# An attention and expert kernel whose front is reordered: dense weights ahead of x's later chunks, one cut on VectorE, DRAM arrays kept by partition

## The chip, the cores and the metric

The kernel runs on one core of a Trainium2 chip. The time is the device time of one execution in microseconds (us). Engines: PE is TensorE (PEld its weight loads), DVE is VectorE, ACT is ScalarE, POOL is GpSimd, SP is SyncE; SPq, ACTq and POOLq are their sequencers, which issue the DMAs.

## The reference

```python
x = L0_attn_x                              # (16, 256, 128)
xn = _layernorm(x, axis=-1)
# attention: 16 heads of 8, LoRA of rank 8 on q, k, v
q, k, v = (xn @ W.T + xn @ Bm.T @ A.T * 2 for each)
s = q k / sqrt(8) + slopes * (i - j) + causal mask
s = (softmax(s) v) @ Wp.T
# experts: 8, the first largest router logit chooses one for each token
h = relu((xn * mask_i) @ W1[i] + b1[i]);  out += h @ W2[i] + b2[i]
return x + s * silu(out)
```

## The kernel before

The 4096 tokens are 32 tiles of 128 rows (NT = 32), two to a batch; there are 16 batches. Five programs, one for each engine, are written out by hand and meet in semaphores; nothing is reordered. A planner (`bank_uses`) only deals out the PSUM banks, four that DVE empties and three that ACT empties, in the order of use.

**Front.** SP loads x in five chunks: tiles 0 to 3, 4 to 7, 8 to 15, 16 to 23, and later 24 to 31 (semaphores x_in0 to x_in4). ACT issues lora and the dense weights (dense_in). PE fills its time with matmuls on zeros (`warm`, line 1127), then forms the LoRA products (line 1132), from which DVE makes w_eff and w_v (line 859). DVE takes each tile's statistics (`moments`, line 796, one instruction a tile) and turns them into rstd and nmr in three groups (`statistics`: tiles 0 to 3, 4 to 15, 16 to 31). Tiles are normalised by DVE, ACT or POOL (NORM_VEC, NORM_ACT, the rest), turned by PE (`turn`, line 1146) and kept (`keep_xT`, ACT line 618 or DVE line 908), projected to q and k (`project`, line 1153) and to v (line 1160).

**Three cuts.** q and k of a batch are cut into three bf16 parts: ACT takes the first (line 624), DVE the remainder (line 847), ACT the second part (line 630), POOL the third (`third_part`, line 503). SP and ACT copy the parts by DMA into qk_stack (lines 409, 371, 377), whose rows also hold constant rows (line 381). Nothing is scored before the last copy of a batch has landed (`stack_ready`).

**Row maxima.** A batch has 11 units (UNITS). For batches 0 and 1 PE scores each unit (lines 1220, 1228) and DVE takes its row maxima (`unit_max`, line 802), with the rest of the statistics, the remainders of batches 2 and 3 and the router logits in between (MOMENTS_FIRST, PROJECT_FIRST, LOGITS_FIRST; `remainder` waits for `project`). In batch 1's run group 2 of the statistics is woven between the maxima (`between`, STATISTICS_FIRST).

**Loop.** Then 16 iterations score batch i (line 1240) and the maxima of batch i+2, exponentiate on ACT (line 741), multiply by v (line 1292), turn and project the result. Meanwhile tokens are ranked by expert; POOL gathers normalised rows from DRAM (line 516) by `from_row`, PE runs 39 expert tiles, and POOL scatters their rows to DRAM (line 530) by `token_of`. At the end SP loads them back, they are gated, multiplied and added to x, and stored (line 452; the last two tiles at line 486).

## Time and profile before

| | us |
|---|---|
| median of 3 runs | 311.3 |
| lowest, highest | 310.02, 312.48 |
| the profiled execution | 307.4 |
| its span in the trace | 305.5 |
| PE busy in the span | 288.2 |
| DVE busy in the span | 214.4 |

The span is the part of the execution that the trace covers; 1.9 us lie around it. All instants below count from its start. A busy PE is not PE at its peak: the columns of a matmul take twice as long at the lower of its two clock levels (1.2 GHz) as at the upper (2.4 GHz).

### The profile page before, as it was taken

How to read it: one execution, taken by the hardware profiler on the slowest of the kernel's cores; microseconds unless marked ns; L12 is line 12 of the kernel's file. 1: busy time of each engine (PE TensorE's matmuls, PEld its weight loads, DVE VectorE, ACT ScalarE, POOL GpSimd, SP SyncE). 2: the span in 40 equal slices, each digit the busy share in tenths (PEclk: the TensorE clock that was granted, in tenths of full speed). 3: DMA queues.
4: the chain of work that ended last, by engine and by line, in shares of the span. 5: the costliest groups of instructions: out<-in, count | busy, mean ns of one | idle time of the engine just before them, and what ended most of it. 6: DMA issues, size and time to landing. Idle time of an engine off the chain costs nothing.

```text
span 305.5 us, 13101 instructions
## 1 busy us (share of the span) xinstructions
PE 288.2 (94%) x5319; PEld 220.9 (72%) x5319; DVE 214.4 (70%) x482; ACT 206.8 (68%) x379; POOL 133.8 (44%) x211
## 2 busy tenths in 40 slices
PE   7989999889798999999999999999999999999893
PEld 3646557758475887888788788878888888876652
DVE  4596897799995665665757576585766667574883
ACT  2343164566568787788778778777778877578981
POOL 3243363114146467646654655655556542141000
PEclk9999999999999999999999999999999999999996
DMA  7689479681224132413313142231414213008532
GB/s 195 164 220 204 122 222 296 217 249 44 59 58 124 47 105 67 118 50 94 81 54 106 51 118 60 76 85 50 123 42 106 79 49 88 28 24 244 146 105 69
DMA packets 46811, 33.89 MB, mean 111 GB/s; under 512 B 5048, under 2 KB 44216, under 8 KB 46624
## 3 DMA queue, kind: packets, MB, share of 16 engines
q1 hardware_dynamic: 42520, 26.80, 32.7%
q0 software_dynamic: 2496, 5.12, 6.1%
q10 hardware_dynamic: 1736, 1.14, 1.7%
q8 instruction: 43, 0.70, 1.0%
q14 instruction: 16, 0.13, 0.1%
HBM read 13.17 MB, written 6.75 MB: 65 GB/s over the span
## 4 chain that ended last, share of the span: by engine, by line
PE 72%; DVE 13%; ACT 4%; DMA 3%; issue 3%; POOL 2%; SPq 1%; ACTq 0%; DVEq 0%; POOLq 0%
PE bank L1342 13%; PE bank L1350 11%; PE bank L1240 11%; PE bank L1292 11%; DVE row_max L802 6%; PE bank L1248 3%; PE bank L1326 3%; PE bank L1153 3%; PE bank L1160 3%; PE bank L1312 3%; DVE w_slots L966 3%; ACT probs L741 2%; PE bank L1334 2%; PE bank L1169 2%; PE bank L1220 2%
## 5 line engine op out<-in xcount | busy, mean ns | idle before, releaser
L802 DVE TENSOR_REDUCE row_max<-bank 128x2 f32<-128x512 f32 (+3 forms) x176 | 105.9, 636 | 21.6 <-PE bank L1228 17.4
L741 ACT ACTIVATE probs<-bank 128x512 f32<-128x512 f32 (+1 forms) x176 | 90.0, 560 | 33.6 <-PE bank L1248 32.9
L1240 PE MATMUL bank<-qk_stack 64*64 64x64 bf16 (+3 forms) x1024 | 60.4, 235 | 3.5 <-DVE row_max L802 1.8
L1220 PE MATMUL bank<-qk_stack 64*64 64x64 bf16 (+3 forms) x1024 | 61.1, 235 | 0.9 <-DMA qk_stack<-parts 0.9
L516 POOL DMA_INDIRECT xs_slot<-normalised_rows,from_row x39 | 38.5, 987 | 41.3 <-PE bank L1248 32.7
L1024 DVE TENSOR_TENSOR hT<-bank,w_slots 128x512 f32<-128x512 f32 x39 | 27.0, 691 | 33.5 <-PE bank L1342 33.5
L530 POOL DMA_INDIRECT expert_rows<-y_slot,token_of x39 | 38.6, 991 | 24.9 <-DVE y_slot L1030 15.0
L1240 PEld LDWEIGHTS bank<-qk_stack 64*64 64x64 bf16 x1024 | 33.9, 107 | 19.7 <-issue 7.3
L717 ACT ACTIVATE w_slots<-w_all 128x1156 f32 x39 | 45.5, 1168 | 3.5 <-issue 1.2
L1292 PE MATMUL bank<-probs,v_diag 128*32 128x64 f32 (+3 forms) x1024 | 45.3, 304 | 0.4 <-issue 0.3
L1342 PE MATMUL bank<-xsT_slot,w_slots 128*128 128x128 f32 x312 | 44.3, 285 | 0.0
L1248 PE MATMUL bank<-cb 64*64 64x128 bf16 (+2 forms) x352 | 43.2, 241 | 0.0
L1228 PE MATMUL bank<-cb 64*64 64x128 bf16 (+2 forms) x352 | 43.0, 241 | 0.0
L1350 PE MATMUL bank<-w_slots,hT 128*128 128x128 f32 x312 | 41.3, 276 | 0.0
L1342 PEld LDWEIGHTS bank<-xsT_slot,w_slots 128*128 128x128 f32 x312 | 37.8, 192 | 2.4 <-issue 0.5
L1350 PEld LDWEIGHTS bank<-w_slots,hT 128*128 128x128 f32 x312 | 38.0, 192 | 0.1
L1220 PEld LDWEIGHTS bank<-qk_stack 64*64 64x64 bf16 x1024 | 33.4, 107 | 5.4 <-issue 5.1
L503 POOL TENSOR_TENSOR parts<-rem,parts 128x512 bf16<-128x512 f32 x16 | 18.5, 1159 | 37.1 <-ACT parts L630 37.1
L1292 PEld LDWEIGHTS bank<-probs,v_diag 128*32 128x32 f32 x1024 | 24.8, 109 | 11.3 <-issue 0.7
L1248 PEld LDWEIGHTS bank<-cb 64*64 64x64 bf16 x352 | 19.7, 107 | 0.0
L1228 PEld LDWEIGHTS bank<-cb 64*64 64x64 bf16 x352 | 19.5, 107 | 0.0
L1127 PE MATMUL bank<-zeros 128*128 128x512 bf16 x49 | 16.6, 444 | 2.3 <-POOL zeros L493 1.0
(134 smaller groups left out, 374.7 us busy)
## 6 DMA issues: line engine op xcount, KB each, us to landing
qk_stack<-parts SPq DMA_DIRECT2D x120, 64.0 KB, 2.0
qk_stack<-parts SPq DMA_DIRECT2D x32, 128.0 KB, 2.4
w_all<-w_experts SPq DMA_DIRECT2D x8, 512.0 KB, 6.0
normalised_rows<-xn_all SPq DMA_DIRECT2D x4, 512.0 KB, 7.2
xn_all<-expert_rows SPq DMA_DIRECT2D x8, 256.0 KB, 5.3
out<-xn_all SPq DMA_DIRECT2D x7, 256.0 KB, 2.3
x_all<-x SPq DMA_DIRECT2D x3, 512.0 KB, 7.5
xs_slot<-normalised_rows,from_row POOLq DMA_INDIRECT x39, 2.9
```

The lines of the kernel that those rows point to most:

```text
L516: pool.indirect_dma_start(xs_slot[:, q % 2, t % 4, :], None, xn_dram[:, :], bass.IndirectOffsetOnAxis(from_row[:, t:t + 1], axis=0)).then_ ...
L530: pool.indirect_dma_start(y_dram[:, :], bass.IndirectOffsetOnAxis(token_of[:, t:t + 1], axis=0), y_slot[:, t % 3, :], None).then_inc(S[f"y ...
L717: act.activation(w_slot[t % 3], w_all[:, bass.ds(e, 1), :].rearrange("p o f -> p (o f)"), ACT.Copy).then_inc(S["w_done"], 1)
L741: act.activation(probs[:, m % PROBS, 0:w], bank[:, 0:w], ACT.Exp).then_inc(emptied, 1)
L802: dve.tensor_reduce(row_max[b % 2][:, n, pairs[0]:pairs[-1] + 1], bank[:, 0:ln_u * len(pairs)].rearrange("p (c k) -> p c k", k=ln_u), AX.X ...
L1220: pe.matmul(bank[to, c * ln_u:(c + 1) * ln_u], q[rows, p, n * BLK:(n + 1) * BLK], k[rows, p, 0:(n + 1) * BLK], start=(c == 0), stop=False, ...
L1228: last = pe.matmul(bank[to, 0:ln_u * len(pairs)].rearrange("p (c k) -> p c k", k=ln_u)[:, :, n * BLK:], ident_b[rows, rows], mask_qk[rows] ...
L1240: pe.matmul(bank[rows, c * ln_u:(c + 1) * ln_u], k[rows, p, kb * BLK:(kb + 1) * BLK], q[rows, p, kb * BLK:], start=(c == 0), stop=False, s ...
L1248: last = pe.matmul(bank[rows, 0:ln_u * len(pairs)].rearrange("p (c k) -> p c k", k=ln_u)[:, :, 0:BLK], ident_b[rows, rows], mask_kq[rows]. ...
L1292: last = pe.matmul(pv_bank[32 * j:32 * j + 32, half * T + kb * BLK:(half + 1) * T], v_diag[b % 2][:, kb, p, :], probs[:, (b * NU + w) % PR ...
L1342: last = pe.matmul(bank[:, c * P:(c + 1) * P], w_slot[t % 3][:, c * P:(c + 1) * P], xsT_slot[:, t // 4 % 2, t % 4, :], start=(c == 0), sto ...
L1350: last = pe.matmul(bank[:, 0:D], hT[:, t % 2, c, :], w_slot[t % 3][:, W2 + c * D:W2 + (c + 1) * D], start=(c == 0), stop=(c == NC_H - 1))
```

## The change

- SP waits for the dense weights before it issues x's chunk 1 and all that stands behind it.
- The constant rows of stack slot 0 are issued by ACT behind normalise(1) instead of at its start; tile 1 is normalised by ACT and tile 2 by DVE.
- `statistics` has one small instruction less in each group.
- PE fills with 12 matmuls instead of 10; w_v is formed last and has its own wait.
- Batch 0's third part goes from POOL to DVE, between the statistics of tiles 10 and 11.
- Tiles 16 to 19 get their statistics ahead of remainder(1); the later ones follow one unit each, so that one is left for batch 1's run, where group 2 starts behind unit 0 instead of unit 4.
- remainder(2) and remainder(3) stand one unit later; ACT's deviation(2) stands ahead of max_rows(0).
- x, out, the normalised rows and the expert rows lie in DRAM by partition: row p * 32 + n instead of n * 128 + p. The ids follow.

```diff
-NORM_VEC, NORM_ACT = (0, 1), (2, 4, 5)
+NORM_VEC, NORM_ACT = (0, 2), (1, 4, 5)
...
-MOMENTS_FIRST = {(0, u): (16 + u,) for u in range(NU)} | {(1, u): (16 + NU + u,) for u in range(16 - NU)}
-STATISTICS_FIRST = 16 - NU
+MOMENTS_FIRST = {(0, u): (20 + u,) for u in range(NU)} | {(1, 0): (31,)}
+STATISTICS_FIRST = 1
...
-    x_tiles = x.rearrange("b (j p) d -> p (b j) d", p=P)
-    out_tiles = out.rearrange("b (j p) d -> p (b j) d", p=P)
+    x_tiles, out_tiles = x, out
...
-    xn_tiles = xn_dram.rearrange("(n p) d -> p n d", p=P)
+    xn_tiles = xn_dram.rearrange("(p n) d -> p n d", p=P)
...
-    y_tiles = y_dram[0:NT * P].rearrange("(n p) d -> p n d", p=P)
+    y_tiles = y_dram[0:NT * P].rearrange("(p n) d -> p n d", p=P)
...
             sp.dma_start(cf[:, 0:P], const_f32[:, 0:P]).then_inc(S["ident_in"], 16)
+            sp.wait_ge(S["dense_in"], 32)
             load_x(1, 4, 8)
...
-            third_part(0)
+            pool.wait_ge(S["part3_done"], 1)
             third_part(1)
...
-            load_const_rows(act, 0, 0, 1)
-
...
-            normalise(2)
+            normalise(1)
+            load_const_rows(act, 0, 0, 1)
             keep_xT(0)
...
             second_part(3)
+            deviation(2)
             max_rows(0)
             first_max_rows()
-            deviation(2)
...
-                follow(dve.tensor_tensor(ln[:, 6, g], ln[:, 6, g], ln[:, 1, g], ALU.mult), group, 5)
-                follow(dve.tensor_scalar(ln[:, 6, g], ln[:, 6, g], -0.5, 1.5, ALU.mult, ALU.add), group, 6)
-                follow(dve.tensor_tensor(rstd[:, g], ln[:, 5, g], ln[:, 6, g], ALU.mult), group, 7)
+                follow(dve.scalar_tensor_tensor(ln[:, 6, g], ln[:, 6, g], -0.5, ln[:, 1, g], ALU.mult, ALU.mult), group, 5)
+                follow(dve.scalar_tensor_tensor(rstd[:, g], ln[:, 6, g], 1.5, ln[:, 5, g], ALU.add, ALU.mult), group, 7)
...
             moments(1, 4, 8)
             remainder(0)
-            then(moments(2, 8, 16))
+            moments(2, 8, 11)
+            dve.wait_ge(S["part2_done"], 1)
+            dve.tensor_tensor(parts[:, 0, 2], rem[:, 0], parts[:, 0, 1], ALU.subtract).then_inc(S["part3_done"], 1)
+            moments(2, 11, 16)
+            then(moments(3, 16, 20))
             remainder(1)
             statistics(1)
...
-                    if b == 0 and u in PROJECT_FIRST:
-                        remainder(PROJECT_FIRST[u])
+                    if b == 0 and u - 1 in PROJECT_FIRST:
+                        remainder(PROJECT_FIRST[u - 1])
...
-            warm(10, vec_bank[3])
+            warm(12, vec_bank[3])
...
             project(1)
+            pe.wait_ge(S["w_eff_done"], 2)
             project_v(0)
```

On SP, the first loads (x_all is x, cf and cb are the constants), before:

```order
L390 DMA x_all<-x 128x4x128
L393 DMA cf<-const_f 128x128
L390 DMA x_all<-x 128x4x128
L395 DMA cb<-const_bf 128x384
L390 DMA x_all<-x 128x8x128
```

and after:

```order
L389 DMA x_all<-x 128x512
L392 DMA cf<-const_f 128x128
L389 DMA x_all<-x 128x512 [waits dense_in]
L395 DMA cb<-const_bf 128x384
L389 DMA x_all<-x 128x1024
```

The loads keep their order, but from the second chunk of x on they stand behind dense_in, and each now moves one run for each partition.

On DVE, from remainder(0) to the first operation of statistics(1) (rem is the remainder, BN_STATS a tile's statistics), before:

```order
L847 TENSOR_TENSOR rem<-bank,parts 128x512 [waits part1_done,vec_full0]
L796 BN_STATS stats<-x_all 128x6 [waits x_in2]
L796 BN_STATS stats<-x_all 128x6 x7
L847 TENSOR_TENSOR rem<-bank,parts 128x512 [waits part1_done,vec_full1,dve_seq]
L820 TENSOR_TENSOR ln<-stats 128x12
```

and after:

```order
L845 TENSOR_TENSOR rem<-bank,parts 128x512 [waits part1_done,vec_full0]
L795 BN_STATS stats<-x_all 128x6 [waits x_in2]
L795 BN_STATS stats<-x_all 128x6 x2
L864 TENSOR_TENSOR parts<-rem,parts 128x512 [waits part2_done]
L795 BN_STATS stats<-x_all 128x6 [waits x_in2]
L795 BN_STATS stats<-x_all 128x6 x4
L795 BN_STATS stats<-x_all 128x6 [waits x_in3]
L795 BN_STATS stats<-x_all 128x6 x3
L845 TENSOR_TENSOR rem<-bank,parts 128x512 [waits part1_done,vec_full1,dve_seq]
```

The third part stands behind the wait for x's chunk 2, and four more tiles' statistics stand ahead of the second remainder.

On DVE, around units 6 and 7 of batch 0's maxima, before:

```order
L802 TENSOR_REDUCE row_max<-bank 128x2 [waits vec_full2]
L796 BN_STATS stats<-x_all 128x6 [waits x_in3]
L847 TENSOR_TENSOR rem<-bank,parts 128x512 [waits part3_done,part1_done,vec_full3]
L802 TENSOR_REDUCE row_max<-bank 128x2 [waits vec_full0]
L796 BN_STATS stats<-x_all 128x6 [waits x_in3]
```

and after:

```order
L801 TENSOR_REDUCE row_max<-bank 128x2 [waits vec_full2]
L795 BN_STATS stats<-x_all 128x6 [waits x_in4]
L801 TENSOR_REDUCE row_max<-bank 128x2 [waits vec_full0]
L795 BN_STATS stats<-x_all 128x6 [waits x_in4]
L845 TENSOR_TENSOR rem<-bank,parts 128x512 [waits part3_done,part1_done,vec_full3]
```

remainder(2) moved behind unit 7's maximum and its statistics, which now read x's last chunk.

## Rows read from the trace of the kernel before

**Rows 1.** The page: busy time of the engines, and the chain by engine.
```profile
PE 288.2 (94%) x5319; PEld 220.9 (72%) x5319; DVE 214.4 (70%) x482; ACT 206.8 (68%) x379; POOL 133.8 (44%) x211
...
PE 72%; DVE 13%; ACT 4%; DMA 3%; issue 3%; POOL 2%; SPq 1%; ACTq 0%; DVEq 0%; POOLq 0%
```

**Rows 2.** The chain of waits, 0 to 20 us: start us, us, what.
```profile
1.39 4.71 DMA dense<-w_dense
...
6.14 1.64 PE bank L1132 x6
7.79 0.96 PE bank L1127 x2
...
9.74 2.06 PE bank L1153 x4
...
12.45 0.64 SPq L409
...
15.73 0.02 SPq L369
...
15.79 2.29 DMA qk_stack<-parts
```

**Rows 3.** PE's timeline: start us, us, line, operation, tiles, count.
```profile
1.01 4.45 PE L1127 MATMUL bank<-zeros 128*128 128x512 bf16 x10 [1.01 <-POOL zeros L493]
...
13.94 3.41 PE L1127 MATMUL bank<-zeros 128*128 128x512 bf16 x15
...
43.20 1.13 PE L1153 MATMUL bank<-xnT_all,w_eff 128*128 128x256 f32 x4
```

**Rows 4.** Windows, 9.5 to 10 us: busy by engine, granted clock, DMA, GB/s.
```profile
9.50:10.00 0.50, 0.36 (x2) 0.29 (x2) 0.06 (x1) 0.46 (x2) 0.00 (x0) 1.00 1.14 297
```

**Rows 5.** The timeline of all engines, 0 to 20 us.
```profile
1.87 1.28 ACTq L381 DMA_DIRECT2D qk_stack<-const_rows  x2
...
6.95 0.16 DVE L836 SCALAR_TENSOR_TENSOR nmr<-ln,rstd 128x4 f32<-128x4 f32 x1
...
13.96 1.16 POOL L503 TENSOR_TENSOR parts<-rem,parts 128x512 bf16<-128x512 f32 x1 [2.59 <-ACT parts L630]
...
15.44 0.69 DVE L847 TENSOR_TENSOR rem<-bank,parts 128x512 f32<-128x512 f32 x1 [0.67 <-ACT parts L624]
...
18.91 0.69 DVE L802 TENSOR_REDUCE row_max<-bank 128x2 f32<-128x512 f32 x1
```

**Rows 6.** The same timeline, 24 to 30 us.
```profile
24.02 0.28 DVE L796 BATCH_NORM_STATS2 stats<-x_all 128x6 f32<-128x128 f32 x1
...
25.29 0.69 DVE L847 TENSOR_TENSOR rem<-bank,parts 128x512 f32<-128x512 f32 x1 [0.98 <-PE bank L1153]
...
26.02 0.62 ACT L630 ACTIVATE parts<-rem 128x512 bf16<-128x512 f32 x1
...
27.86 1.74 POOL L506 TENSOR_SCALAR xn_all<-x_all,rstd,nmr 128x128 f32<-128x128 f32 x4
```

**Rows 7.** The chain in the second run: a tile's statistics, a small operation.
```profile
36.37 0.20 DVE stats L796
...
39.69 0.18 DVE ln L834
```

**Rows 8.** PE's timeline at 44.9 and 48 us: what PE waited for.
```profile
44.90 0.27 PE L1240 MATMUL bank<-qk_stack 64*64 64x192 bf16 x2 [0.23 <-DVE row_max L802]
...
48.05 0.27 PE L1240 MATMUL bank<-qk_stack 64*64 64x192 bf16 x2 [0.58 <-DVE xnT_all L908]
```

**Rows 9.** The page: DMA issues, count, KB each, us to landing; waits for the gathers.
```profile
w_all<-w_experts SPq DMA_DIRECT2D x8, 512.0 KB, 6.0
...
x_all<-x SPq DMA_DIRECT2D x3, 512.0 KB, 7.5
xs_slot<-normalised_rows,from_row POOLq DMA_INDIRECT x39, 2.9
...
  DMA xs_slot<-normalised_rows,from_row: 1.8, 3
```

**Rows 10.** The timeline's last row.
```profile
303.24 0.37 SPq L486 DMA_DIRECT2D out<-xn_all  x1
```

More of the change, by code:

```diff
@@ L855, in _ @@
             dve.wait_ge(S["lora_ps"], 1)
[L856 to L860 removed]
+            for n in range(2):
+                last = dve.scalar_tensor_tensor(w_eff[:, n, :], pv_bank[:, n * P:(n + 1) * P], LORA_SCALE, w_raw[:, n, :], ALU.mult, ALU.add)
             then(last)
             dve.tensor_scalar(w_eff[:, 0, :], w_eff[:, 0, :], float(DH) ** -0.5, None, ALU.mult).then_inc(S["w_eff_done"], 1)
+            dve.scalar_tensor_tensor(w_v[:, :, :], pv_bank[:, 2 * P:3 * P].rearrange("p (a x) -> p a x", a=2), LORA_SCALE,
+                                     w_raw[:, 2, :].rearrange("p (a x) -> p a x", a=2), ALU.mult, ALU.add).then_inc(S["w_eff_done"], 1)
             moments(1, 4, 8)
             remainder(0)
[L865 removed]
+            moments(2, 8, 11)
[3 more added lines that the diff above has]
+            then(moments(3, 16, 20))
             remainder(1)
@@ L971, in keep_ids @@
                 bank, emptied = wait_vec_full(dve, "ids")
-                then(dve.tensor_copy(r40[:, 0, :], bank[:, 0:SLOT_ROWS]))
-                dve.scalar_tensor_tensor(r40[:, 1, :], bank[:, SLOT_ROWS:2 * SLOT_ROWS], float(P), r40[:, 0, :], ALU.mult, ALU.add).then_inc(emptied, 1)
+                then(dve.tensor_copy(r40[:, 0, :], bank[:, SLOT_ROWS:2 * SLOT_ROWS]))
+                dve.scalar_tensor_tensor(r40[:, 1, :], bank[:, 0:SLOT_ROWS], float(NT), r40[:, 0, :], ALU.mult, ALU.add).then_inc(emptied, 1)
                 wait_vec_emptied(dve, "ids")
-                dve.tensor_scalar(from_row[:, :], r40[:, 1, :], -1.0, 0.0, ALU.add, ALU.max).then_inc(S["rows_done"], 1)
+                dve.tensor_scalar(from_row[:, :], r40[:, 1, :], -float(NT), 0.0, ALU.add, ALU.max).then_inc(S["rows_done"], 1)
                 then(dve.scalar_tensor_tensor(r40[:, 0, :], r40[:, 1, :], 0.0, spare_ids, ALU.is_equal, ALU.mult))
-                dve.scalar_tensor_tensor(token_of[:, :], r40[:, 1, :], -1.0, r40[:, 0, :], ALU.add, ALU.add).then_inc(S["tokens_done"], 1)
+                dve.scalar_tensor_tensor(token_of[:, :], r40[:, 1, :], -float(NT), r40[:, 0, :], ALU.add, ALU.add).then_inc(S["tokens_done"], 1)
             def tile_experts():
```

13 lines of the change are left out of this document (4 added, 9 removed).

## The prediction

> **What bounds the kernel now.** I read the page first, then the chain of waits from the start, then the timelines of the engines around it. The page says that PE works 94% of the span and carries 72% of the chain, DVE 13% [rows 1]. The main loop, from about 42 us to 298 us, is therefore PE's and none of its matmuls is touched. What the change can move is the point at which this loop gets going, and the last store. So the question is what ends last in the front.
>
> The chain of the front [rows 2] has three links. The dense weights land at 6.10, then PE does the lora products (6.14, 1.64 us), two filling matmuls, the turns of x and the projection of batch 0 (9.74, 2.06 us). SP issues five copies into the stack from 12.45 on, one after the other, and the last lands at 18.08. Then PE scores and VectorE takes maxima, and up to 48 us the two hold each other.
>
> In the first link PE runs slowly. Ten 128x512 filling matmuls take 4.45 us, 0.44 each, and fifteen of the same shape from 13.94 on take 3.41, 0.23 each; the projection of batch 0 takes 2.06 us and the same pair at 43.20 takes 1.13 [rows 2, 3]. The granted clock stands at 1.00 there [rows 4], but the durations are those of the lower level (1.2 GHz) up to about 13 us and of the upper one (2.4 GHz) after it. Before it rose, PE had a hole of 0.69 us (5.46 to 6.14, the wait for the dense weights), small products, and then about 3.6 us of dense projections.
>
> **The change, part by part: to the first store.** Two more filling matmuls carry PE to 1.01 + 12 x 0.44 = 6.3 us, and SP holds back x's later chunks, so that dense comes well before that. The hole goes, and the lora products begin at 6.3 in place of 6.14: by itself this loses 0.2. The gain is what an unbroken 5.3 us of dense matmuls may do: I take it that the clock rises near 6 us. Then lora takes half of 1.64, two fillings 0.45, the first turn half of its time: the first turn is done at 7.9. ScalarE is ready for it a little later. One small operation less in the statistics (0.20 from start to start) puts nmr at 7.11 - 0.2 = 6.9 [rows 5]; the two constant-row DMAs now stand behind normalise(1) on ScalarE and hold its queue 1.28 us [rows 5], to 8.2. This is the price of moving them: keep_xT(0) waits 0.3 us for them. From 8.2: copy 0.39, a gap of 0.15, projection 1.1, first part 0.61, so SP's first store goes at 10.5 in place of 12.45, 1.95 us earlier. The five issues (3.3 us) and the landing (2.29) stay, so the stack is ready 1.95 earlier too, at 16.1.
>
> **Third part on VectorE.** Nothing in the trace does this subtraction on VectorE. The nearest row is the remainder, 0.69 us for the same 128x512 with one operand in PSUM; GpSimd takes 1.16 [rows 5]. I take 0.65, bounds 0.4 and 1.16. On the path it gains nothing: GpSimd ended at 15.12, and SP came to that copy at 15.73. It adds waits to VectorE, for x's third chunk and for part 2, and behind them stand the other statistics, remainder(1) and all maxima. The sum on VectorE: remainder(0) at 10.5 to 11.2, ScalarE's second part to 11.85, third part to 12.5, nine statistics at 0.205 to 14.35, and remainder(1) there in place of 15.44 (1.1 earlier). With an operation less in statistics(1), the first maximum starts at 17.6, 1.3 earlier than 18.91 [rows 5].
>
> **Remainder(2) behind unit 7.** PE reaches project(2) 1.95 us earlier, since the bank it needs is emptied in time. VectorE ends unit 6 with its statistics at 24.3 - 1.3 = 23.0, unit 7's maximum and statistics take 0.66, and remainder(2) starts at 23.7 in place of 25.29: 1.6 earlier. The row then is as before: second part on ScalarE, third part and four normalisations on GpSimd, and the turn that PE waits for at 29.6 [rows 6]. The second run of maxima starts 1.6 us earlier.
>
> **Statistics out of the second run.** There VectorE does five tile statistics, and afterwards one: 4 x 0.20 = 0.8 us; and a small operation of 0.20 goes [rows 7]. VectorE gains 1.0 and stands at 1.6 + 1.0 = 2.6 us earlier when it frees xnT_all, for which PE waited 0.58 before 48.05 [rows 8]. PE, whose own work is unchanged, can gain only 1.6 plus its waits on VectorE there, 0.58 and 0.23: 2.4. The smaller holds: 2.4 us. Deviation(2) ahead of max_rows(0) costs ScalarE 0.3 us in an idle stretch: nothing.
>
> **DRAM layout.** x's loads, the kept rows, the y loads and the stores move 2 or 4 KB a piece in place of 512 B. The 512 KB of an expert, in 4 KB pieces, land in 6.0 us, the 512 KB of x in 7.5 [rows 9]. None of these is waited for in the loop: at the start x's first chunk is, and at the end the last store (issued at 303.24) [rows 10]. I count 0 to 0.5 for both together, and nothing in the sum. Against it: gathered rows now lie 16 KB apart or more; a gather lands in 2.9 us [rows 9], and PE waited for three of them for 1.8 us in all, so half a microsecond may be lost. The keep_ids arithmetic is as long as before.
>
> The page "DMA: Bandwidth & Descriptors" of the Trainium skill, Specifications, says that pieces of 512 B already run at line rate. By that the layout gives nothing; the two rows differ by 1.5 us, but with different company, so the trace does not settle it. The sum is the same either way.
>
> **Sum.** Against the profiled execution (307.4 us, span 305.5) the change gives 305.0. The three timed runs have a median of 311.3, 3.9 above it; the front is the same program in them, so I carry the difference over: 311.3 - 2.4 = 308.9.
>
> **Rivals.** (A) Forecast, 308.9, chance 0.55. Its own range is 308.1 to 310.
>
> (B) The clock does not rise early. For it: in the trace ten fillings did not raise it, and from 6.14 to 9.6 an almost unbroken stretch of lora products, fillings and turns didn't either. Then lora starts 0.2 late, the first store goes at 12.65, and VectorE carries 0.65 + 0.8 us more before remainder(1), less 0.3 that it waited: it starts at 16.5, 1.1 late; the first maximum 0.9 late; remainder(2) 0.6 late; the second run gives back 1.0 on VectorE, 0.8 on PE. Net -0.2: 311.1. Chance 0.22.
>
> The Trainium skill's page "TensorE: Matmul & The Clock Gate", Part 1, says that the low clock is the default and sustained matmuls release it, at a point that varies from run to run. That makes A and B a matter of the single run: the trace here is one draw, and a median of runs may lie between them.
>
> (C) Slower. SP's wait for dense holds x's chunks 1 to 3, the masks and the constants. If dense still lands at 6.1, chunk 2 is issued at about 7.1 and lands, at x's 7.5 us, at 14.6. VectorE needs it at 11.2, ahead of the third part. Then the third part ends at 15.9, SP's last copy has no gain, remainder(1) starts at 17.7, the first maximum at 21.1, 2.2 late, remainder(2) 1.8 late, and less PE's 0.8 of waits the loop is 1.0 late: 312.3. It decides from the point where chunk 2 lands after about 13.5. Against it: before, dense shared the engines with x's chunks 1 and 2, the masks and the constant rows, which now come later. Chance 0.08.
>
> (D) More than forecast. x's first chunk, alone with dense and in 2 KB pieces, lands 0.5 us earlier, which moves nmr and ScalarE's DMA issues with it, and the gathers and stores give 0.5: 2.4 + 1.0 = 3.4, so 307.9. Chance 0.15.
>
> **Numbers.** 1% is 3.1 us, about what a measurement can tell. Below 308.2 lie D and a quarter of A: 0.28. Above 314.4 only a bad C: 0.02. Within: 0.70. The range takes D's and B's ends: 307.6 to 311.6.
>
> **What the profile after will show.** Filling matmuls at the start: 12, and the lora products right behind them; the projection of batch 0 in 1.1 us (A) or 2.0 (B). First store at 10.5; first scores at 16.1; first maximum at 17.6; a VectorE third part of 0.65; remainder(2) at 23.7; loop's 0.58 us wait on xnT_all gone; span 303.1. VectorE idle on x's chunk ahead of the third part would show C. The prediction fails if the clock stays low, or if another wait of 1 us appears between 18 and 48 us.

## The result: 1.1% slower, and the profile after

| | kernel before | changed kernel |
|---|---|---|
| executions timed, alternating | 20 | 20 |
| median | 311.39 | 314.45 |
| lowest | 306.63 | 309.28 |
| the profiled execution, its span | 307.4, 305.5 | 316.44, 314.6 |

The ratio is 1.0112, 95% interval 1.0064 to 1.0161. The forecast was 308.9 and its range ended at 311.6; slower by over 1% had a chance of 0.02. The ratios of this text leave out executions that stand over 1.5% above the fastest of their kernel; where means over executions are given, they hold all of them except three far off (1433, 522 and 324 us).

The rows of the changed kernel follow in the order of those of before. First the page: busy time, the granted clock in 40 slices, the chain by engine. They answer to [rows 1].

```profile
PE 293.7 (93%) x5321; PEld 223.8 (71%) x5321; DVE 214.0 (68%) x480; ACT 206.2 (66%) x379; POOL 132.8 (42%) x210
...
PEclk9955999997899999999999999999999999999997
...
PE 74%; DVE 10%; ACT 5%; DMA 4%; issue 3%; POOL 2%; SPq 1%; ACTq 0%; DVEq 0%; POOLq 0%
```

The clock line is the first thing to read: slices 3 and 4 (15.7 to 31.5 us) stand at 5. The trace's record of the clock has it low from 16.8 to 30.4 us, again from 74.8 to 81.6, and at the end from 310.3. The record of the kernel before begins with the rise at 13.2 us and has it low only from 299.9 on.

The chain of waits of the front, start us, us, what; it answers to [rows 2].

```profile
7.43 0.81 ACTq L380
...
8.82 1.12 PE bank L1154 x4
...
10.58 0.65 SPq L409
...
14.24 0.05 issue
14.31 0.05 issue
14.36 3.81 DMA qk_stack<-parts
18.17 0.14 issue
18.31 0.63 PE bank L1221 x4
```

PE's timeline, with the idle time ahead of a group in brackets; it answers to [rows 3] and [rows 8].

```profile
1.01 5.30 PE L1128 MATMUL bank<-zeros 128*128 128x512 bf16 x12 [1.01 <-POOL zeros L493]
...
6.25 1.06 PE L1133 MATMUL bank<-hT 8*128 8x128 f32 x6
...
11.33 3.41 PE L1128 MATMUL bank<-zeros 128*128 128x512 bf16 x15
...
18.31 0.63 PE L1221 MATMUL bank<-qk_stack 64*64 64x256 bf16 x4 [3.56 <-DMA qk_stack<-parts]
...
27.25 2.07 PE L1154 MATMUL bank<-xnT_all,w_eff 128*128 128x256 f32 x4
...
53.12 0.27 PE L1241 MATMUL bank<-qk_stack 64*64 64x192 bf16 x2 [0.57 <-DVE xnT_all L909]
...
75.27 0.85 PE L1293 MATMUL bank<-probs,v_diag 128*32 128x192 f32 x5 [2.13 <-issue]
```

The first half of the forecast is there. The twelve filling matmuls lead into the lora products without a hole, the pair of projections takes 1.12 us in place of 2.06, and the first store is issued at 10.58, forecast 10.5. The second half is not. The last copy lands at 18.17, where it landed at 18.08 before: its issue came 1.4 us earlier, and the landing took 3.81 us in place of 2.29. And because PE came to its fifteen filling matmuls 2.6 us earlier, they were over at 14.74, where they had lasted to 17.35. PE then stood still for 3.56 us in place of 0.86.

The windows say what this cost: busy us of PE, PEld, DVE, ACT, POOL with instruction counts, granted clock, DMA share, GB/s.

```profile
4.00:6.00 2.00, 2.00 (x6) 0.58 (x4) 1.59 (x12) 0.30 (x1) 0.00 (x0) 1.00 0.12 23
...
14.70:18.30 3.60, 0.04 (x1) 0.02 (x1) 3.16 (x14) 0.93 (x2) 1.15 (x1) 0.79 1.02 273
18.30:30.00 11.70, 11.69 (x68) 7.04 (x69) 6.75 (x20) 2.83 (x6) 2.59 (x6) 0.50 0.73 146
```

PE did next to nothing from 14.7 to 18.3, the clock fell in it, and in the next 11.7 us PE was busy all the time at 0.50. A four-matmul group of the maxima then takes 0.63 us (0.41 in e1, with the clock up) and a pair of projections 2.07. The first row shows another thing: from 4 to 6 us the DMA engines moved 23 GB/s, since SP sat in its wait until 4.91. The kernel before has, in the same stretch,

```profile
4.00:6.00 2.00, 1.46 (x4) 0.27 (x2) 1.63 (x11) 0.30 (x1) 0.00 (x0) 1.00 1.11 277
```

and the changed kernel then has, in the stretch in which SP issues the first copies into the stack,

```profile
10.00:12.00 2.00, 2.00 (x24) 1.22 (x23) 1.28 (x4) 1.17 (x2) 0.00 (x0) 1.00 0.95 274
```

where the kernel before moves 129 GB/s, and 22 in its own stretch of the first copies, from 12 to 14 us. x's chunks are still under way here.

The other engines' timeline in the front, and then from 30 us on (it answers to [rows 5] and [rows 6]).

```profile
4.91 0.33 SPq L389 DMA_DIRECT2D x_all<-x  x1
...
6.57 0.16 DVE L834 SCALAR_TENSOR_TENSOR nmr<-ln,rstd 128x4 f32<-128x4 f32 x1
...
12.04 0.69 DVE L864 TENSOR_TENSOR parts<-rem,parts 128x512 bf16<-128x512 f32 x1
...
14.66 0.87 DVE L795 BATCH_NORM_STATS2 stats<-x_all 128x6 f32<-128x128 f32 x4 [0.95 <-DMA x_all<-x]
...
15.57 0.69 DVE L845 TENSOR_TENSOR rem<-bank,parts 128x512 f32<-128x512 f32 x1
...
19.15 0.69 DVE L801 TENSOR_REDUCE row_max<-bank 128x2 f32<-128x512 f32 x1 [0.29 <-PE bank L1229]
...
30.61 0.68 DVE L845 TENSOR_TENSOR rem<-bank,parts 128x512 f32<-128x512 f32 x1
...
33.16 1.74 POOL L506 TENSOR_SCALAR xn_all<-x_all,rstd,nmr 128x128 f32<-128x128 f32 x4
```

Remainder(2), forecast at 23.7, comes at 30.61; POOL's four normalisations at 33.16 in place of 27.86. Who waits for whom between 18 and 48 us is in the view of waits (us in total, times, longest):

```profile
DVE row_max L801 <- PE bank L1229: 6.7, 12, 1.8
```

and in the kernel before, where the pair waited once:

```profile
DVE row_max L802 <- PE bank L1228: 0.4, 1, 0.4
```

There VectorE was the slower of the two in this stretch; now it is PE. The loop starts at 46.95 in place of 41.55, and the row at 48.05 [rows 8] stands at 53.12: 5.1 us. From there to the end it is 4.1 us more (261.5 against 257.4), and these lie at 72 to 82 us: a pause of PE of 2.13 us put down to "issue" ahead of 75.27, and 6.8 us of low clock around it. Such a pause is not the change's alone: 1.6 to 2.6 us of it, at 57 to 80 us, stand in ten of the 20 profiles of this text, three of them of the kernel before with one thing altered (e3, e9, e12), each with a low stretch of the clock beside it. One of them, of `e2_no_dense_wait` below:

```profile
72.01 0.52 PE L1292 MATMUL bank<-probs,v_diag 128*32 128x192 f32 x5 [1.86 <-issue]
```

But all ten are among the 13 profiles whose clock had fallen between 16 and 45 us already, and none of the other seven has it. So a change that adds falls in the front may add this pause too; what ties the two was not tested.

The page's DMA issues (count, KB each, us to landing), and the last store; they answer to [rows 9] and [rows 10].

```profile
w_all<-w_experts SPq DMA_DIRECT2D x8, 512.0 KB, 5.6
normalised_rows<-xn_all SPq DMA_DIRECT2D x4, 512.0 KB, 7.5
...
x_all<-x SPq DMA_DIRECT2D x3, 512.0 KB, 4.9
xs_slot<-normalised_rows,from_row POOLq DMA_INDIRECT x39, 2.8
```

```profile
312.51 0.33 SPq L486 DMA_DIRECT2D out<-xn_all  x1
```

### The profile page after: what moved, and what is told of

It is laid out like the page before. It is cut to its first block, busy times and chain, and to the rows that moved or that the text cites. A ratio compares the mean times of both kernels' runs of the same rounds, so it can differ in the third digit from the quotient of the medians.

```text
span 314.6 us, 13103 instructions
## 1 busy us (share of the span) xinstructions
PE 293.7 (93%) x5321; PEld 223.8 (71%) x5321; DVE 214.0 (68%) x480; ACT 206.2 (66%) x379; POOL 132.8 (42%) x210
## 4 chain that ended last, share of the span: by engine, by line
PE 74%; DVE 10%; ACT 5%; DMA 4%; issue 3%; POOL 2%; SPq 1%; ACTq 0%; DVEq 0%; POOLq 0%
PE bank L1343 13%; PE bank L1351 11%; PE bank L1241 11%; PE bank L1293 11%; DVE row_max L801 4%; PE bank L1221 3%; PE bank L1249 3%; PE bank L1327 3%; PE bank L1154 3%; PE bank L1161 3%; PE bank L1313 3%; ACT probs L740 2%; PE bank L1170 2%; PE bank L1128 2%; PE bank L1335 2%
## 5 line engine op out<-in xcount | busy, mean ns | idle before, releaser
L1221 PE MATMUL bank<-qk_stack 64*64 64x64 bf16 (+3 forms) x1024 | 62.8, 239 | 3.6 <-DMA qk_stack<-parts 3.6
L1241 PE MATMUL bank<-qk_stack 64*64 64x64 bf16 (+3 forms) x1024 | 60.5, 235 | 2.8 <-ACT probs L740 1.0
L1025 DVE TENSOR_TENSOR hT<-bank,w_slots 128x512 f32<-128x512 f32 x39 | 27.0, 691 | 32.9 <-PE bank L1343 32.7
L503 POOL TENSOR_TENSOR parts<-rem,parts 128x512 bf16<-128x512 f32 x15 | 17.4, 1159 | 45.2 <-ACT parts L628 45.2
L1128 PE MATMUL bank<-zeros 128*128 128x512 bf16 x51 | 17.7, 455 | 2.3 <-POOL zeros L493 1.0
```

The lines of the kernel that those rows point to most:

```text
L1221: pe.matmul(bank[to, c * ln_u:(c + 1) * ln_u], q[rows, p, n * BLK:(n + 1) * BLK], k[rows, p, 0:(n + 1) * BLK], start=(c == 0), stop=False, ...
L1241: pe.matmul(bank[rows, c * ln_u:(c + 1) * ln_u], k[rows, p, kb * BLK:(kb + 1) * BLK], q[rows, p, kb * BLK:], start=(c == 0), stop=False, s ...
```

## The experiments

Theory: two faults. **Idle:** the fifteen filling matmuls now end 3.6 us ahead of the stack, PE stands still, the clock falls, and the first run of maxima goes at half rate. **Load order:** held back behind the dense weights, x's chunks 2 and 3 come into the time of the copies into the stack, VectorE waits for chunk 3, and the copies land late. Rivals: the twelve filling matmuls at the start do it, or the DRAM layout does. In the expectations of the first group, theory 1 is the idle, theory 2 the load order and theory 3 the layout; "idle matmuls" is their other name for the filling matmuls. Unless said otherwise an experiment starts from the changed kernel and leaves the rest of it as it is.

The runs come in five groups. Kernels of one group ran on one chip, alternating with the kernel before. On two chips every kernel took about 5% longer, the kernel before too, so only ratios and differences to it are compared across groups. Profiles are of one execution each.

**First group (kernel before: median 326.52).**

`e1_bridge`: more filling matmuls behind the projection.

```diff
-            warm(15, pv_bank)
+            warm(31, pv_bank)
```

> The changed kernel with 31 filling matmuls instead of 15 behind project_v(0). In the profile after, PE stopped at 14.7 us, the clock fell at about 17 and came back at 30.4, and everything on PE between 18.3 and 30.8 took twice as long. Theory 1 (the clock falls in the wait for the stack): with PE kept busy to about 18 us the granted clock stays at 1.00 from 18 to 31 us, the turn that follows POOL's four normalisations comes at 29.5 to 30 instead of 34.96, and the time drops by 4 to 5 us, to 0.99 to 1.00 of the kernel before. Theory 2 (x's chunks and the first copies land late because SP waits for dense): the fillers change nothing about the landing at 18.2, and the kernel stays at 1.01 unless the clock is the cost. Theory 3 (the DRAM layout costs in the loop): stays at 1.01.

Measured: ratio 1.0041, 0.9987 to 1.0095. In its profile the clock is up from 6.2 to 316.9 us without a break. PE's timeline at the stack:

```profile
14.68 3.40 PE L1128 MATMUL bank<-zeros 128*128 128x512 bf16 x15
18.01 0.41 PE L1221 MATMUL bank<-qk_stack 64*64 64x256 bf16 x4
```

and the same stretch as above in its windows:

```profile
18.30:30.00 11.70, 10.93 (x108) 7.35 (x103) 9.41 (x25) 4.08 (x8) 5.40 (x11) 1.00 0.84 190
```

In the 11.7 us PE does 108 instructions where the changed kernel does 68. The loop starts at 41.77 (41.55 before, 46.95 changed). So in these profiles the idle is the 5 us; and since PE still comes to its first scores at 18.0, nothing of the forecast gain is there either.

`e2_no_dense_wait`: SP's wait for the dense weights taken out.

```diff
-            sp.wait_ge(S["dense_in"], 32)
```

> The changed kernel without SP's wait for the dense weights. Theory 2 (the wait leaves the DMA engines idle from 4 to 6 us and x's chunk 3 and the first copies land late): VectorE's 0.95 us wait for chunk 3 goes, the last copy of batch 0 lands 2.3 us behind its issue instead of 3.8, and the first scores start at about 16.7 instead of 18.3; the gap on PE shrinks to 2 us and the clock falls less often: ratio 0.995 to 1.005. Theory 1 alone (the clock, with the gap for its cause) expects the same only if the gap shrinks; if the dense weights land so late that the clock does not rise early, project(0) takes 2.0 us and the front is as before. Theory 3: no change, 1.01.

Measured: ratio 1.0102, 1.0008 to 1.0196. Its PE timeline:

```profile
16.07 0.41 PE L1220 MATMUL bank<-qk_stack 64*64 64x256 bf16 x4 [1.50 <-DMA qk_stack<-parts]
```

First scores at 16.07 and the first maximum at 17.68: the forecast had 16.1 and 17.6. No wait of VectorE for a chunk is left. The load order theory holds for the landing. The time does not follow, for the clock was low from 21.9 to 25.3 and from 32.1 to 39.0 us, and the loop started at 44.20 (41.55 in the kernel before).

`e3_warm12`: the kernel before with 12 filling matmuls at the start in place of 10, nothing else.

```diff
-            warm(10, vec_bank[3])
+            warm(12, vec_bank[3])
```

> The kernel before with 12 filling matmuls at its start instead of 10 and nothing else. Theory 1: in most executions the clock rises at 6 to 8 us instead of 13, project(0) takes 1.1 us, the fillers behind project_v end about 2 us earlier, PE stops for 2.5 us or more before the stack is ready, and in part of the executions the clock falls there: ratio 1.000 to 1.010, with more spread than before. Theory 2 or 3 (neither touches this kernel): the ratio is 0.993 to 1.000, since the front is shorter and nothing is lost.

Measured: ratio 0.9986, 0.9914 to 1.0058. They alone do nothing that can be measured, so they are not the loss. In its profile the dense weights landed late (PE waited 1.24 us, to 7.55) and the clock rose at 6.9, fell at 10.3 and rose at 13.7.

`e4_old_layout`: the changed kernel with x, out and the two DRAM arrays laid out as before.

```diff
-    x_tiles, out_tiles = x, out
+    x_tiles = x.rearrange("b (j p) d -> p (b j) d", p=P)
+    out_tiles = out.rearrange("b (j p) d -> p (b j) d", p=P)
...
-    xn_tiles = xn_dram.rearrange("(p n) d -> p n d", p=P)
+    xn_tiles = xn_dram.rearrange("(n p) d -> p n d", p=P)
```

> The changed kernel with x, out, the normalised rows and the expert rows in DRAM as in the kernel before. Theory 1 and 2: within 0.5% of the changed kernel (ratio 1.005 to 1.02); x's chunks in pieces of 512 B land somewhat later, so if anything slower. Theory 3 (gathered and scattered rows 16 KB apart cost in the loop, and the pause of 2.1 us on PE at 73 us comes from it): ratio below 1.003.

Measured: ratio 1.0230, 1.0114 to 1.0345. The layout is not the loss: without it the loss is larger. VectorE's and PE's rows:

```profile
15.05 0.87 DVE L796 BATCH_NORM_STATS2 stats<-x_all 128x6 f32<-128x128 f32 x4 [1.35 <-DMA x_all<-x]
```

```profile
18.61 0.63 PE L1222 MATMUL bank<-qk_stack 64*64 64x256 bf16 x4 [3.93 <-DMA qk_stack<-parts]
```

The chunks come later still (1.35 us of waiting for chunk 3), PE is idle longer, and the clock was low for 30.8 us, from 18.2 to 49.0.

**Second group (kernel before: median 311.81), with the changed kernel itself on the same chip.**

> The changed kernel itself, unchanged, so that it stands on the same chip as the three beside it. Its first timing gave a ratio to the kernel before of 1.011; 1.005 to 1.02 is expected here, with the granted clock down from about 17 us to about 30 us, the loop's start at about 47 us and the wait for the stack (3.5 us on PE at about 18.3 us).

Measured: ratio 1.0049, 0.9989 to 1.0109; first scores at 17.73 after 3.14 us of idle, clock low from 19.0 to 29.2, loop's start 45.58. The fall is as forecast; the ratio stands at the lower edge of what was expected, and the wait and the loop's start are 0.4 and 1.4 us below it.

`e6_bridge_again` is `e1_bridge` unchanged.

> The changed kernel with 31 idle matmuls in place of 15 behind project_v(0), a second time, now with the changed kernel on the same chip. If the loss is the clock's fall behind the idle matmuls (PE stops 3.56 us, then 12 us at half rate), the loop starts at 41.8 us as before and the time is 3 to 5 us below the changed kernel's, thus within 1% of the kernel before. Rival: the first timing's closeness to the kernel before was that chip's; then the time is within 1 us of the changed kernel's.

Measured: ratio 0.9942, 0.9881 to 1.0003; 3.1 us below the changed kernel by the medians (310.65, 313.71), 3.3 ± 1.7 by the means of all executions. In its profile nothing fell at 17 us, but the clock was low from 30.6 to 40.8 us, and the loop started at 45.94, not at the 41.8 expected. So a fall around 30 us exists without the idle ahead of the stack. PE was busy 16.96 of the 17 us from 30 to 47. The profiles alone would not tell e6 from e5 (45.94, 45.58); the timed executions do.

`e7_x_early_bridge`: both mended.

```diff
-            sp.wait_ge(S["dense_in"], 32)
...
-            warm(15, pv_bank)
+            warm(23, pv_bank)
```

> The changed kernel without SP's wait for the dense weights and with 23 idle matmuls behind project_v(0). The stack then lands at 16.1 us, as in the run without the wait, and PE is busy up to it. Theory (clock and load order are the two faults): first scores at 16.1 us, no fall of the clock before 30 us, the loop starts at 39.5 to 40.5 us, and the time is 1 to 2 us below the kernel before. Rival: with the earlier stack PE runs ahead of the work that it needs in the first run of maxima, has holes there, and the clock falls between 20 and 40 us all the same: loop's start 43 to 45 us and a time 1 to 3 us above the kernel before.

Measured: ratio 0.9891, 0.9833 to 0.9950, all six executions at or below 310.21. The profiled one was not the clean one expected: the clock was low from 8.9 to 12.3 (the dense weights came 1.06 us late, PE's lora products at 7.04) and from 32.8 to 39.7, and the loop started at 44.87. The time is better than its own profile.

`e8_x_early_bridge_all`: one filling matmul more in each of seven units.

```diff
-WARM_FIRST = [(0, u) for u in (0, 1, 2, 10)] + [(1, u) for u in range(NU)]
+WARM_FIRST = [(b, u) for b in range(2) for u in range(NU)]
```

> The kernel with the early x and 23 idle matmuls, and one idle matmul more behind each unit of batch 0's first maxima that had none (7 more, 0.22 us each where PE waits anyway). If holes in the first run of maxima are what lets the clock fall after 20 us, it stays up here, the loop starts at 39.5 to 40.5 us and the time is 1 to 2 us below the kernel before. Rival: PE is not idle there but waits for no one, so the seven matmuls (1.5 us) lie on the path: loop's start 1 to 1.5 us later than without them.

Measured: ratio 0.9950, 0.9884 to 1.0017; low again from 32.8 to 39.6, loop's start 45.86, 1.0 later than without them. The rival holds: these matmuls lie on the path and keep nothing up.

**Third group (kernel before: median 311.49).**

`e9_before_layout`: the kernel before with the new layout alone.

> The kernel before with the new DRAM layout alone (x, out, the normalised rows and the experts' rows kept by partition, 4 KB pieces in place of 512 B). The prediction held this part at 0. The run of the changed kernel with the old layout stood 1.2% above the changed kernel (ratio to the kernel before 1.023 against 1.011), so if that is the layout's own worth, this one stands at a ratio of 0.985 to 0.992. Rival: that difference came through the clock (x's chunks later, PE idle longer behind its idle matmuls), which the kernel before does not have in this form; then the ratio is 0.997 to 1.003, with x's transfers nearer to 5 us than to 7.5.

Measured: median 311.67 over 12 executions, 304.59 to 314.44; mean 310.9 against 311.6. The ratio of 0.9843 (0.9790 to 0.9895) rests on its three quickest executions only; by all twelve it is 0.7 us below the kernel before, plus or minus 0.9. The rival holds: no gain that can be told. Its profile is the odd one: with the old ten filling matmuls the clock rose at 5.6 us, not at 13.2. x's chunks took 7.8 us to land in it (median), so they were no quicker than in the kernel before.

`e10_fill_turn`: `e7` and two filling matmuls ahead of turn(4), where PE waited 0.53 us for GpSimd in e7.

```diff
                     if (b, u) in TURN_FIRST:
+                        warm(2 * (u == 9), pv_bank)
                         turn(TURN_FIRST[b, u])
```

> The kernel with the early x and 23 idle matmuls, and two idle matmuls (0.45 us) more ahead of turn(4), where PE had waited 0.53 us for GpSimd at about 28.9 us before its clock fell at 32.8 us. If that hole is what lets the clock fall there, it stays up to the end of the first maxima, the loop starts 3 us earlier (41.5 to 42 us in place of 44.9) and the time is 1 to 2 us below the same kernel without them. Rival: the fall follows the stretch of small products (transposes, the router's 8 columns), in which PE is busy; then the clock falls at 31 to 33 us as before and the time is the same within 1 us.

Measured: ratio 0.9872, 0.9825 to 0.9919, mean 307.9 over five. Its profile has the clock up from 6.0 to 299.5. PE's timeline:

```profile
16.45 0.41 PE L1220 MATMUL bank<-qk_stack 64*64 64x256 bf16 x4
...
26.70 0.60 PE L1127 MATMUL bank<-zeros 128*128 128x512 bf16 x2
27.30 1.53 PE L1146 MATMUL bank<-cf,xn_all 128*128 128x128 f32 x4
```

The first maximum comes at 17.90, the loop starts at 40.49, the row of [rows 8] stands at 46.65 and the span is 303.15; the forecast was 303.1. The sixth execution, 522 us, is the one left out.

`e11_x_early_again` is `e7_x_early_bridge` unchanged.

> The kernel with the early x and 23 idle matmuls a second time, beside the others: 0.989 of the kernel before in its first timing; 0.985 to 0.995 is expected, if the gain is the kernel's and not that timing's.

Measured: ratio 0.9866 (0.9801 to 0.9930) from the quickest ones, but a median of 312.79; two of five executions at 305.3 and 308.8, three at 312.7 to 313.9 (the sixth, at 324.49, is left out). The gain of the second group is not secured by this.

`e12_before_bridge`: the kernel before with 19 filling matmuls in place of 15.

> The kernel before with 19 idle matmuls in place of 15 behind project_v(0), which fills the 0.86 us that PE waited there for the stack. If more idle matmuls were the whole gain of the kernel with the early x, this one gains as much (ratio near 0.99). By the theory it does not: the kernel before has no fall of the clock there in its trace, first scores and first maximum stay at 18.2 and 18.9 us, and the ratio is 0.997 to 1.003.

Measured: median 311.56, mean 0.8 below the kernel before, plus or minus 1.5 (the ratio of 0.9830, 0.9774 to 0.9885, is of its two quickest). More filling alone is no gain that shows.

**Fourth group (kernel before: median 329.37).** What is each kept part worth once the idle is gone?

`e13_third_on_pool`: `e10` with batch 0's third part back on GpSimd.

```diff
-            pool.wait_ge(S["part3_done"], 1)
+            third_part(0)
             third_part(1)
...
-            dve.wait_ge(S["part2_done"], 1)
-            dve.tensor_tensor(parts[:, 0, 2], rem[:, 0], parts[:, 0, 1], ALU.subtract).then_inc(S["part3_done"], 1)
```

> The kernel with the early x, 23 idle matmuls and two ahead of turn(4), and the first third part back on GpSimd, where it took 1.16 us in the kernel before (0.69 us on VectorE). The prediction held that this move gains 0.65 us on the stack's parts and nothing on the path that ends last. If that holds, the last of SP's copies for stack 0 is issued at most 0.5 us later, first scores come at 16.3 to 17 us, and the time is that of the kernel with the part on VectorE within 1 us. Rival: the copies wait for the part, first scores at 17 us or later, and 0.5 to 1 us of it reaches the end.

(The 0.65 us were the prediction's length of the operation, not a gain.)

Measured: ratio 1.0026, 0.9956 to 1.0096; mean 326.4 against 327.8 (± 0.9) for the kernel with the part on VectorE, `e15` below. First scores no later (16.34, behind the filling matmuls in both). Its VectorE rows, and then those of `e10`:

```profile
13.65 0.69 DVE L844 TENSOR_TENSOR rem<-bank,parts 128x512 f32<-128x512 f32 x1
...
16.92 0.69 DVE L800 TENSOR_REDUCE row_max<-bank 128x2 f32<-128x512 f32 x1
```

```profile
14.57 0.69 DVE L844 TENSOR_TENSOR rem<-bank,parts 128x512 f32<-128x512 f32 x1
...
17.90 0.69 DVE L800 TENSOR_REDUCE row_max<-bank 128x2 f32<-128x512 f32 x1
```

The part on VectorE gives the stack nothing and delays the first maximum by 0.98 us, of which 0.40 is left at the loop's start (40.09, 40.49) and at the row of [rows 8] (46.26, 46.65).

`e14_fill_old_layout`: `e10` with the old layout.

> The same kernel (early x, 23 idle matmuls, two ahead of turn(4)) with x, out, the normalised rows and the experts' rows in the old DRAM layout (512 B pieces). The prediction held the layout at 0, and the kernel before with the new layout alone stood within 1 us of the kernel before. If the layout is worth nothing by itself, this one stands within 1 us of the kernel with the new layout, though with x's chunks landing later (VectorE waits for chunk 2 or 3). Rival: the earlier x needs the short transfers; then VectorE waits 1 us or more for a chunk, first scores are later than 17 us, behind the 23 idle matmuls the clock falls, and the time is 2 to 4 us higher.

Measured: ratio 1.0073, 0.9995 to 1.0151; mean 328.2 against 327.8. No wait of VectorE for a chunk, first scores at 16.24, clock up from 4.4 to 318.4. With x early the layout is worth nothing that can be told in the time, though x's chunks took 6.9 us to land, against 5.9 in e10. What `e4` lost on top of the changed kernel would then have come through the chunks' wait and the clock; no run takes the two apart.

`e15_fill_turn_again` is `e10` unchanged.

> The version that was best so far (early x, 23 idle matmuls, two ahead of turn(4)), a second time: a ratio to the kernel before of 0.985 to 0.992 is expected. In the executions without a fall of the clock before the end it stands 2.3 us below the kernel before's such ones (span 303.1 us).

Measured: ratio 1.0036, 0.9966 to 1.0105; by all executions 1.2 us below the kernel before, plus or minus 0.9. Not the 0.985 to 0.992 expected. Its profile had the clock low from 9.0 to 12.4, 32.9 to 39.7 and 60.2 to 70.4.

`e16_after_third_time` is the changed kernel.

> The changed kernel itself once more, beside the three: a ratio of 1.005 to 1.015, and at least 12 us of low clock in each of its executions (one fall in the front in all of them).

Measured: median 333.73, 1.3% above the kernel before's, six executions, 326.92 to 336.56, too few and too wide for an interval. In all six the clock was low for 12.4 us or more. In the profiled one it did not fall in the idle ahead of the stack (2.56 us there, first scores 17.21) but from 30.1 to 40.3 and from 60.8 to 71.1. So the idle does not bring the fall every time.

**Fifth group (kernel before: median 309.18).**

`e17_one_chunk_early`: chunk 1 ahead of SP's wait, 25 filling matmuls, two ahead of turn(4).

```diff
-            sp.wait_ge(S["dense_in"], 32)
             load_x(1, 4, 8)
+            sp.wait_ge(S["dense_in"], 32)
```

> The changed kernel with x's chunk 1 loaded ahead of SP's wait for the dense weights and chunks 2 and 3 behind it, 25 idle matmuls in place of 15 and two ahead of turn(4). Theory: the dense weights come in time as with the wait (lora products at 6.3 us, no fall of the clock at 9 us), and only chunk 3 can still be late; first scores between 16.1 and 17.7 us, mean low-clock time 8 to 14 us an execution, and a ratio to the kernel before of 0.985 to 0.995. Rival: what makes the stack late is chunks 2 and 3 beside the copies; then first scores come at 17.5 to 18.2 us as in the changed kernel, the clock falls behind the idle matmuls in some executions, and the ratio is 1.00 to 1.01.

Measured: ratio 1.0044, 0.9988 to 1.0100, above the 0.985 to 0.995 expected; median 308.21 against 309.18. Dense weights in time (lora products at 6.24), no wait for chunk 3, first scores at 16.85 right behind the filling matmuls, first maximum 17.87, loop 40.59, span 302.91, the shortest here. By this one profile it was chunk 1 held back, and with it all that is issued behind it, that made the copies late (SP issued chunks 2 and 3 0.55 us earlier, at 5.21 and 6.16); chunks 2 and 3 behind the dense weights did no harm.

`e18_fill_turn_third` is `e10` unchanged.

> The kernel without the wait (early x, 23 idle matmuls, two ahead of turn(4)) a third time, beside it: mean low-clock time 11 to 14 us, ratio 0.985 to 0.997. Its weak point is that the dense weights share the DMA engines with x's chunks: lora products at 5.9 to 6.9 us and, in some executions, a fall of the clock from 9 to 12.4 us.

Measured: ratio 1.0107, 1.0029 to 1.0184, where 0.985 to 0.997 was expected; median 309.79. Its weak point showed: PE waited 1.59 us for the dense weights and the clock was low from 8.0 to 11.4.

## What the executions say together

Each execution comes with its mean granted clock. The level is 0.5 or 1, so 2 x (1 - clock) x span is the time at the low level (the stretch ahead of the first rise is not in it: the kernel before's profile has 0.991, which is 5.5 us, the stretch from 299.9 to its end). One line per kernel and chip with a common slope, fitted to the 247 executions of the five groups, has a slope of 0.387 us for each us of low clock, plus or minus 0.011 (standard error), and leaves 1.1 us of scatter, of 2.5 without it. Differences to the kernel before on the same chip (± is one standard error):

| kernel | mean low-clock us, against before | mean time, us | at equal low clock, us |
|---|---|---|---|
| changed, first timing | 23.6, not recorded | +4.0 ± 0.8 | - |
| changed, second group | 23.0, 18.4 | +2.6 ± 1.3 | +0.8 ± 0.5 |
| changed, fourth group | 23.8, 16.6 | +4.0 ± 1.5 | +1.3 ± 0.5 |
| e1, e6 (31 filling matmuls) | 11.6, 14.8; 14.1, 18.4 | -0.3 ± 1.0; -0.8 ± 1.3 | +1.0 ± 0.4; +0.9 ± 0.5 |
| e2 (no wait); e3 (before, twelve at the start) | 18.9, 14.8; 16.5, 14.8 | +2.1 ± 1.0; +0.4 ± 1.0 | +0.6 ± 0.5; -0.2 ± 0.4 |
| e4 (old layout) | 30.1, 14.8 | +8.2 ± 1.5 | +2.3 ± 0.5 |
| e7, e11 (x early, 23 filling) | 11.6, 18.4; 17.1, 19.3 | -3.4 ± 0.9; -0.9 ± 1.6 | -0.7 ± 0.5; -0.1 ± 0.5 |
| e8 (seven more) | 14.8, 18.4 | -0.8 ± 1.1 | +0.6 ± 0.5 |
| e10 (and two at turn(4)); e15; e18 | 10.8, 19.3; 13.5, 16.6; 13.8, 12.9 | -3.7 ± 1.4; -1.2 ± 0.9; +1.4 ± 1.2 | -0.4; 0.0; +1.1 (± 0.5) |
| e13 (third part on GpSimd) | 11.3, 16.6 | -2.7 ± 0.7 | -0.6 ± 0.4 |
| e14 (e10, old layout) | 14.1, 16.6 | -0.9 ± 0.9 | +0.1 ± 0.4 |
| e17 (one chunk early) | 9.7, 12.9 | -0.2 ± 1.0 | +1.0 ± 0.4 |
| e9 (before, new layout); e12 (before, 19 filling) | 16.2, 19.3; 17.6, 19.3 | -0.7 ± 0.9; -0.8 ± 1.5 | +0.4 ± 0.4; -0.1 ± 0.5 |

Of the changed kernel's 31 executions (19 of them from the first timing, 12 from the groups) none had less than 12 us of low clock; of the kernel before's 97 in the groups, 24 had. So of the changed kernel's 2.6 and 4.0 us, 0.387 x 4.6 = 1.8 and 0.387 x 7.2 = 2.8 are the clock, and about 1 is the rest. The stack that lands no earlier while more work stands ahead of VectorE's first maximum would fit this rest, but that is not shown: the last column gives the same kernel (e10, e15, e18) -0.4, 0.0 and +1.1, so a difference of 1 us in it tells little.

That the idle brings the low clock rests on the same figures: with it filled and nothing else altered, e6 has 14.1 us of it where the changed kernel beside it has 23.0, and 0.387 x 8.9 = 3.4 us is the 3.3 us between their mean times.

## Why the prediction was wrong, by its steps

- **The clock rises near 6 us: held** for the changed kernel (6.5; 5.4 and 6.2 in its other profiles). In all 17 profiles with twelve filling matmuls at the start it rose at 4.4 to 6.9 us. That the kernel before does not have this already: only in its profile (13.2) and in e12 (13.1). In e9, with ten, it rose at 5.6. The hole of 0.69 us is not what made it late: e12 had none there (lora products at 5.39, right behind the filling matmuls). The prediction said itself that A and B are matters of the single run, and then took the whole gain against one draw.
- **First store at 10.5: held** (10.58), with its terms: two fillings 0.60 for 0.45, the constant rows hold ScalarE's queue to 8.24 for 8.2, projection 1.12 for 1.1.
- **"The five issues (3.3 us) and the landing (2.29) stay, so the stack is ready 1.95 earlier too, at 16.1": the first step that failed.** The issues took 3.8 (10.58 to 14.36) and the landing 3.81. The change also moved x's chunks into this stretch; the prediction moved them only for VectorE, in rival C. That the chunks are what made the copies late is shown by loading them early: e2 without SP's wait has 16.07, e17 with chunk 1 alone ahead of it at most 16.85.
- **The term that was missing: what PE does between its filling matmuls and the stack.** The prediction moved the projection 1.95 us forward and the filling matmuls behind it with it, and never set their new end (14.7) against the stack. Even by its own 16.1 PE would have stood still for 1.4 us, and e2, where it was 1.5, had its low stretches too. At the real 18.17 it was 3.56. This is the 5.1 us at the row of 53.12, shown for the profile by e1 (loop's start 41.77 without it) and for the time by e6 against e5 (3.3 ± 1.7 us). It is a matter of chance in the single execution: behind 3.14, 3.56 and 3.93 us of idle the clock fell (e5, changed kernel, e4), behind 2.56 (e16) it did not, until 30.1. "The prediction fails if the clock stays low" named the sign, but for the start alone.
- **Rival C**, the late chunk, was right in kind: VectorE waited 0.95 us, for chunk 3 and not for chunk 2. Its price went through the copies into the stack, and its chance of 0.08 was far too small: the wait leaves the DMA engines at 23 GB/s for 2 us and the traffic has to go somewhere.
- **First maximum 17.6, remainder(2) 23.7:** 19.15 and 30.61. In e2 and in e10, without the faults, the first maximum is at 17.68 and 17.90: this term was mis-sized by no more than 0.3.
- **Third part on VectorE, 0.65, nothing on the path:** 0.69, and nothing for the stack; but it delays the first maximum by 0.98 and the loop's start by 0.40 (e13). The prediction had it in VectorE's sum. Whether it reaches the end is open: e13 stands 1.5 ± 0.9 us below e15, 0.6 at equal low clock.
- **"PE ... can gain only 1.6 plus its waits on VectorE there, 0.58 and 0.23":** mis-sized. The 0.57 us wait for xnT_all is there in the changed kernel, and 0.56 in e10 and e17: it belongs to the order of the loop's first iteration and not to a backlog. From loop's start to that row it is 6.50 us before, 6.17 changed, 6.16 in e10 and e17: 0.3 gained, not 0.8.
- **Layout 0: held.** x's chunks land in 4.9 us for 7.5 and nobody gains (e9, e14). The order of the loads has a part in this: like with like they land in 5.9 for 6.9 (e10, e14) and in 7.8 for 7.5 (e9, kernel before). The page "DMA: Bandwidth & Descriptors" of the Trainium skill, Specifications, gives 512 B as the least size for line rate, which would say the same of the total; no run here measured the rate by itself.
- **"The front is the same program in them, so I carry the difference over": failed.** The 3.9 us between profile and median fit falls of the clock, 0.387 us for each us of them (16.2 us in the mean of 97 executions, 5.5 in the profile: 4.1); a change that adds such falls moves the median by more than any profile without them shows.

**Would the forecast have come out without the two faults?** In one execution, yes: e10 has the span 303.15 and e17 302.91 for the forecast 303.1. In the timing, hardly: at equal low clock e17 is 1.0 us above the kernel before on its chip and e10 0.4 below. A version that beats the kernel before for certain was not found; e7, e10 and e13 stood 2.7 to 3.7 us below it in their groups, by all executions, and the repeats e11, e15 and e18 at -0.9, -1.2 and +1.4. Open stays why the clean front's lead of 1.0 to 1.5 us at the loop's start (40.09 to 40.59 in e10, e13, e14 and e17, against 41.55) does not show at equal low clock. One reason would be that the kernel before often has the early rise too (as e9, first maximum at 17.72); there is only one profile of it, and this was not shown.

## What to carry to other kernels

Filling matmuls are sized to a gap: whoever moves their start must also move their end, to the moment at which the next real work is ready, and read the gap behind them in the forecast timeline. A load that is held back for a more urgent one is not removed: look at which transfers it now meets, and hold back as little as does it (here one chunk, e17). And before a gain is taken from one profile, compare its low-clock time with that of the timed runs; here that was 5.5 us in the profile against a mean of 16.

## What the runs showed of the hardware that was not expected

- The clock fell also while PE was busy: in e6 from 30.6 to 40.8 us, with PE busy 10.93 of the 11.7 us from 18.3 to 30 (e1, with the same 10.93, had no fall), in e15 at 32.9 with 9.75 of the 10 us from 22 to 32, and around the same place in e2, e3, e7, e8, e9, e11, e12 and e16. What stands there are four f32 transposes, router products of 8 columns and 64-row products. The page "TensorE: Matmul & The Clock Gate" of the Trainium skill, Part 4, says that transposes do not count as busy in the same way; the place of these falls agrees with that, but the seven profiles without a fall have the same transposes there, and no run here took them away. The advice of the same page of the Trainium skill against idle between bursts ("Why this matters for your kernels") agrees with the fall behind the idle of 3.56, 3.93 and 3.14 us in the changed kernel, e4 and e5.
- It is a matter of the execution: the same kernel (e10, e15, e18) had no fall in one profile, three in another, and one at 8.0 us in the third. Executions of one kernel on one chip differ by 8 us (304.41 to 312.35 for the kernel before in the fifth group), mostly through this: with the low-clock time taken out, 2.5 us of scatter become 1.1.
- Late dense weights cost PE more than their wait: in e3, e7, e8, e15 and e18 PE waited 0.75 to 1.59 us for them, the clock fell at 8.0 to 10.3 us, and the eight matmuls of the projections took 2.67 to 3.61 us in place of 1.97. With SP's wait in place (changed kernel, e1, e4, e5, e6, e16, e17) neither was seen once, which is what the wait is good for. The late weights are not the only way to that fall: in e9 and e11 it came at 9 us with the weights in time.
- A us of low clock goes with 0.387 us of the kernel and not with the 0.5 of the halved rate. That PE waits for others in part of that time anyway, or does work that isn't bound by its clock, would explain it; this was not tested.
